# A metaformer block in software pipeline: DVE's scaling directly behind the statistics, POOL's two additions beside both, ACT's normalised columns as five in two portions

## What is computed

```python
def reference(x, conv_kernel, W1, b1, W2, b2):      # x: (32, 112, 112, 96) f32
    x = x + (conv3x3_depthwise(ln_c(x)) + ln_c(x))  # layer norm over the 96 channels, eps 1e-6
    t = to_tokens(x)
    t = t + ffn(ln_t(t))                            # layer norm over the 96 channels, eps 1e-5
    return from_tokens(t)

def ffn(t):                                         # hidden size 384
    h = relu(q_acc(q_acc(q_mul(t) @ q_mul(W1).T) + q_mul(b1)))
    return q_acc(q_acc(q_mul(h) @ q_mul(W2).T) + q_mul(b2))
```

## Time and profile before

| | before |
|---|---|
| median of 3 runs | 3998.27 us (3997.37 to 4000.93) |
| profiled execution, its own time | 3986.89 us |
| its span (first to last instruction) | 3985.2 us |
| mean granted clock of TensorE | 0.967 of full speed |
| busy: PE, DVE, ACT, POOL | 79%, 91%, 73%, 43% of the span |

### The profile page before, as it was taken

One profiled execution on the slowest core, in us unless ns is written; L12 is line 12 of the kernel. 1 busy time (PEld: TensorE's weight loads), 2 busy tenths in 40 slices (PEclk: granted clock), 3 DMA queues, 4 the chain that ended last, 5 costly groups with the idle time before them and its releaser, 6 DMA issues.

```text
span 3985.2 us, 87474 instructions
## 1 busy us (share of the span) xinstructions
PE 3157.9 (79%) x24902; PEld 2493.7 (63%) x24902; DVE 3609.6 (91%) x12635; ACT 2925.6 (73%) x6204; POOL 1719.3 (43%) x915
## 2 busy tenths in 40 slices
PE   3488888878887888878888787887888888889977
PEld 3376666666666666666666666666666666667744
DVE  6558999999999999999999899998999999999998
ACT  4457777777777777777777777777777777776765
POOL 0003444444444444444444444444444444445555
PEclk9999999999999999999999999999999999999955
DMA  4566666656666666666666666666666666665533
GB/s 135 179 175 182 189 186 189 189 173 189 189 186 187 179 185 189 186 187 189 185 189 184 181 189 186 189 186 174 189 187 189 187 189 190 191 190 171 164 107 92
DMA packets 277355, 714.63 MB, mean 179 GB/s; under 512 B 34809, under 2 KB 34914, under 8 KB 276834
## 3 DMA queue, kind: packets, MB, share of 16 engines
q1 hardware_dynamic: 276834, 708.57, 60.6%
HBM read 539.84 MB, written 168.59 MB: 178 GB/s over the span
## 4 chain that ended last, share of the span: by engine, by line
PE 54%; ACT 31%; issue 7%; DMA 4%; DVE 1%; ACTq 1%; SPq 1%; POOL 0%; POOLq 0%; DVEq 0%
PE conv_ps L390 33%; ACT images L473 14%; PE hid_ps L355 13%; ACT hid L452 9%; PE y_ps L368 7%; ACT y L460 4%; ACT xt L444 4%; DMA band_ring<-bands 3%; DMA xn<-in_x 1%; ACTq L171 1%; DVE stats L593 0%; PE conv_ps L333 0%; PE xt_ps L342 0%; DVE images L574 0%; SPq L270 0%
## 5 line engine op out<-in xcount | busy, mean ns | idle before, releaser
L390 PE MATMUL conv_ps<-images,band_ring 112*112 112x222 f32 (+1 forms) x9216 | 2058.5, 362 | 512.6 <-ACT xt L444 382.1
L390 PEld LDWEIGHTS conv_ps<-images,band_ring 112*112 112x112 f32 x9216 | 1563.0, 178 | 805.6 <-issue 550.8
L452 ACT ACTIVATE hid<-hid_ps 128x896 f16<-128x896 f32 x1344 | 1225.4, 912 | 504.4 <-PE hid_ps L355 504.4
L232 POOL TENSOR_TENSOR xf<-xf,images 112x768 f32<-112x768 f32 x448 | 979.8, 2187 | 1263.8 <-DVE hid L582 893.2
L238 POOL TENSOR_TENSOR xf<-xf,y 112x768 f32<-112x768 f32 x448 | 736.2, 1643 | 997.9 <-DVE y L613 997.9
L637 DVE SCALAR_TENSOR_TENSOR xq<-xf,stats,xt_ps 112x96 fp8e5<-112x96 f32 x3584 | 844.3, 310 | 0.0
L368 PE MATMUL y_ps<-w2t,hid 128*128 128x96 f16 x10752 | 634.7, 211 | 173.9 <-ACT y L460 172.3
L368 PEld LDWEIGHTS y_ps<-w2t,hid 128*128 128x128 f16 x10752 | 554.9, 100 | 329.3 <-ACT y L460 213.3
L473 ACT ACTIVATE images<-xn,neg_mean,rstd 112x96 f32<-112x96 f32 x1792 | 723.0, 544 | 14.3 <-DVE neg_mean L629 14.2
L355 PE MATMUL hid_ps<-xt,w1t 96*128 96x448 fp8e5 x2688 | 694.6, 368 | 27.9 <-ACT xt L444 19.4
L460 ACT ACTIVATE y<-y_ps 112x384 f16<-112x384 f32 x896 | 443.2, 495 | 363.6 <-PE y_ps L368 362.0
(11 more groups left out here) (46 smaller groups left out, 604.3 us busy)
## 6 DMA issues: line engine op xcount, KB each, us to landing
band_ring<-bands SPq DMA_DIRECT2D x768, 294.0 KB, 5.2
xn<-in_x SPq DMA_DIRECT2D x448, 336.0 KB, 3.5
xf<-in_x SPq DMA_DIRECT2D x448, 336.0 KB, 4.8
out<-xf SPq DMA_DIRECT2D x448, 336.0 KB, 3.9
bands<-images SPq DMA_DIRECT2D x4, 3528.0 KB, 13.6
xf<-in_L_ffn_W SPq DMA_DIRECT2D x2, 144.0 KB, 2.8
xf<-in_L_conv_kernel SPq DMA_DIRECT2D x3, 3.4 KB
xf<-in_L_ffn_b SPq DMA_DIRECT2D x1, 42.0 KB, 3.2
```

What stands on the lines that cost most here:

```text
L232: pool.tensor_tensor(x2, x2, images[:, b, i, :, cols].rearrange("p c w -> p w c"), ALU.add).then_inc(with_conv, 1)
L390: mm = pe.matmul(dst[:, :, lo:hi], band_ring[:, n % BAND_RING, PAIR * dx + i, :], images[:, m % 2, :, ch, lo + dx - 1:hi + dx - 1], start= ...
L452: nc.scalar.activation(hid[:, c % 2, TOK * j:TOK * (j + 1)].rearrange("p (u n) -> p u n", u=2), hid_ps[:, k, :, 0:HALF * H], ACT.Identity) ...
```

## The change

Three things are changed. No operation is added or taken out, except that one semaphore is new (`rstd_t_done`).

On DVE, `scale` of the step's own chunk comes directly behind `statistics`, with statistics and reciprocals of the step before; it was done for the next chunk, behind `invert`. `invert` is cut in two: `invert_c` (first layer norm) stands directly behind `scale`, `invert_t` (second layer norm) behind `quantise`. All three `add_bias` of chunk c - 1 stand together, in front of `quantise`. Five columns of the first layer norm are ACT's and three are DVE's (it was four and four).

On POOL, `add_ffn` comes first and takes chunk c - 3 (it was c - 2); it waits until DVE's `normalise` of the step before is done. `add_conv` follows it without a wait for DVE's biases.

On ACT, `deviation` comes first in the step, in front of `copy_xt`; two of the five columns are normalised between `copy_xt` and the first `cast_hid`, the other three between the two halves of `cast_y`. The third `cast_hid` comes in front of the first `cast_y`.

```diff
-ACT_COLS = 4
+ACT_COLS = 5
+ACT_FIRST = 2
...
-                def add_conv(r, c, t):
+                def add_conv(r, c):
...
-                    if ffn_in(t - 1):
-                        wait(pool, hid_biased, J * (LOOP * r + c - FFN_AT))
                     pool.wait_ge(xf_in[e % FFN_RING], dma_count(r, e, FFN_RING))
...
-                def add_ffn(r, c):
-                    e = c - FFN_AT
+                def add_ffn(r, c, t):
+
+                    e = c - 3 - FFN_AT
+                    if norm_in(t - 1):
+                        wait(pool, normed[1], LOOP * r + c - NORM_AT)
                     wait(pool, y_biased, LOOP * r + e + 1)
                     res = xf[0:H, e % FFN_RING]
-                    pool.tensor_tensor(res, res, y[:, c % 2], ALU.add).then_inc(summed, CW)
+                    pool.tensor_tensor(res, res, y[:, e % 2], ALU.add).then_inc(summed, CW)
 
                 def step(r, c, t):
+                    if ffn_in(t - 3):
+                        add_ffn(r, c, t)
                     if ffn_in(t + 2):
-                        add_conv(r, c, t)
-                    if ffn_in(t - 2):
-                        add_ffn(r, c - 2)
+                        add_conv(r, c)
...
-                def normalise(r, c):
+                def normalise(r, c, lo, hi):
                     e = c - NORM_AT
                     b, i, cols = chunk_at(e)
-                    wait(act, neg_done, LOOP * r + e + 1)
-                    wait(act, with_conv, LOOP * r + e - LOOP + 1)
...
+                    if lo == 0:
+                        wait(act, neg_done, LOOP * r + e + 1)
+                        wait(act, with_conv, LOOP * r + e - LOOP + 1)
...
-                    for w in range(ACT_COLS):
+                    for w in range(lo, hi):
...
+                    if ffn_in(t + 1) or norm:
+                        deviation(r, c, t)
                     if now:
                         copy_xt(r, c)
                     save_conv(r, c - 1, t - 1, 3, C)
+                    if norm:
+                        normalise(r, c, 0, ACT_FIRST)
                     if now:
                         cast_hid(r, c, 0)
-                    if ffn_in(t + 1) or norm:
-                        deviation(r, c, t)
                     save_conv(r, c, t, 0, 1)
                     if now:
                         cast_hid(r, c, 1)
                     save_conv(r, c, t, 1, 3)
+                    if now:
+                        cast_hid(r, c, 2)
                     if before:
                         cast_y(r, c - 1, 0)
-                    if now:
-                        cast_hid(r, c, 2)
                     if norm:
-                        normalise(r, c)
+                        normalise(r, c, ACT_FIRST, ACT_COLS)
                     if before:
                         cast_y(r, c - 1, 1)
...
+                def invert_t(r, c, t):
+
+                    wait(dve, xt_copied, LOOP * r + c - FFN_AT + 1 if ffn_in(t) else 0)
+                    wait(dve, std_done, LOOP * r + c - NORM_AT + 1)
+                    dve.reciprocal(rstd_t, std[:, c % 2, 0]).then_inc(rstd_t_done, 1)
...
-                    if before:
-                        add_bias(r, c - 1, 2)
+                    if now:
+
+                        wait(dve, rstd_t_done, LOOP * r + c - FFN_AT + 1)
                     if after or norm:
                         statistics(r, c, t)
...
+                    if now:
+                        scale(r, c)
+                    if norm:
+                        invert_c(r, c)
                     if before:
+                        for j in range(J):
+                            add_bias(r, c - 1, j)
                         quantise(r, c - 1)
-                    if after or norm:
-                        invert(r, c, t)
+                    if after:
+                        invert_t(r, c, t)
                     if ffn_in(t - 2):
                         add_y_bias(r, c - 2)
-                    if after:
-                        scale(r, c)
                     if norm:
                         normalise(r, c)
-                    if now:
-                        add_bias(r, c, 0)
-                        add_bias(r, c, 1)
```

More of the change, by code:

```diff
@@ L139, in metaformer @@
         stats_done, std_done, rstd_done, neg_done = sem("stats_done"), sem("std_done"), sem("rstd_done"), sem("neg_done")
+        rstd_t_done = sem("rstd_t_done")
         normed = [sem("normed_act"), sem("normed_dve")]
@@ L462, in cast_y @@
                                          ACT.Identity).then_inc(y_cast, 1)
-                def normalise(r, c):
+                def normalise(r, c, lo, hi):
                     e = c - NORM_AT
                     b, i, cols = chunk_at(e)
-                    wait(act, neg_done, LOOP * r + e + 1)
-                    wait(act, with_conv, LOOP * r + e - LOOP + 1)
-                    if e == STAGED_FROM:
-                        for s in bands_out:
-                            act.wait_ge(s, 16)
-                    for w in range(ACT_COLS):
+                    if lo == 0:
+                        wait(act, neg_done, LOOP * r + e + 1)
+                        wait(act, with_conv, LOOP * r + e - LOOP + 1)
+                        if e == STAGED_FROM:
+                            for s in bands_out:
+                                act.wait_ge(s, 16)
+                    for w in range(lo, hi):
                         op = nc.scalar.activation(images[:, b, i, :, cols.start + w], xn[:, e % NORM_RING, w, :],
@@ L475, in normalise @@
                                                   scale=rstd[:, c % 2, w:w + 1])
-                    op.then_inc(normed[0], 1)
+                    if hi == ACT_COLS:
+                        op.then_inc(normed[0], 1)
                 def save_conv(r, c, t, lo, hi):
@@ L614, in add_y_bias, with invert_c @@
                                       ALU.add).then_inc(y_biased, 1)
-                def invert(r, c, t):
+                def invert_c(r, c):
                     k = LOOP * r + c - NORM_AT
-                    if ffn_in(t + 1):
-                        wait(dve, xt_copied, LOOP * r + c - FFN_AT + 1 if ffn_in(t) else 0)
                     wait(dve, std_done, k + 1)
[L622 to L626, removed]
-                    dve.wait_ge(rstd_done, k + 1)
[L628 to L631, removed]
+                    dve.reciprocal(rstd[:, c % 2], std[:, c % 2, 1]).then_inc(rstd_done, 1)
+                    dve.wait_ge(rstd_done, k + 1)
+                    dve.scalar_tensor_tensor(out=neg_mean[:, c % 2, :], in0=stats[:, c % 2, 1, :, 1], scalar=-1.0,
+                                             in1=rstd[:, c % 2], op0=ALU.mult, op1=ALU.mult).then_inc(neg_done, 1)
+                def invert_t(r, c, t):
+                    wait(dve, xt_copied, LOOP * r + c - FFN_AT + 1 if ffn_in(t) else 0)
+                    wait(dve, std_done, LOOP * r + c - NORM_AT + 1)
+                    dve.reciprocal(rstd_t, std[:, c % 2, 0]).then_inc(rstd_t_done, 1)
                 def scale(r, c):
-                    e = c + 1 - FFN_AT
+                    e = c - FFN_AT
                     for w in range(CW):
                         op = dve.scalar_tensor_tensor(
-                            out=xq_8[:, (c + 1) % 2, w // 2, 0:C, w % 2], in0=xf[0:H, e % FFN_RING, w, :],
-                            scalar=stats[:, c % 2, 0, w, 1:2], in1=rstd_t[:, w:w + 1].broadcast_to([H, C]),
+                            out=xq_8[:, c % 2, w // 2, 0:C, w % 2], in0=xf[0:H, e % FFN_RING, w, :],
+                            scalar=stats[:, (c - 1) % 2, 0, w, 1:2], in1=rstd_t[:, w:w + 1].broadcast_to([H, C]),
                             op0=ALU.subtract, op1=ALU.mult, saturate=False)
```

3 lines of the change are left out of this document (2 added, 1 removed).

## The result

The changed kernel took 4007.65 us (median of 12 runs, 3997.93 to 4021.2), the kernel before 3997.35 beside it (12 runs). The ratio is 1.0028, with a 95% interval of 1.0015 to 1.0042: **0.28% slower**, where 0.7% faster was forecast. The profiled execution has a span of 4019.5 against 3985.2.

What follows compares the result with a forecast made beforehand. A closed chain through ACT and PE was taken to set the step, with no engine busy throughout. Terms -68 - 6 + 26 + 15 + 5 = -28 from 3998.3 gave 3970 us, range 3905 to 4040.

Steps and rivals of the forecast that it cites:

- 340 steps gain 0.20 each, -68: Loop steps: 8.12 us each instead of 8.32, taking 68 us off.
- The chain: Closed chain through DVE, PE and ACT over two steps: 16.10 us, 8.05 a step, 8.12 in the loop.
- the registers' 0.15: Working out counts in registers costs today's loop step 0.15 us; half was taken for the new chain.
- (c): Rival, chance 0.22: registers cost the loop step in full, 8.20, total 3997; with 0.2 more latency in the chain, 4036.
- The span that I gave for the forecast: 3935 to 3992 us, from unit ends at nothing or full price and a loop step of 8.05 or 8.17.
- The unit's ends: At 13 unit ends POOL's late addition holds up DVE's quantise: 2.0 us each, +26 in all.
- The closing steps: From step 419 on, y's first half stands behind the third cast: 0.27 us for 57 steps, +15.
- the first steps: In the first 28 steps ACT's fifth column lies in the chain: +5 us, at the low end nothing.
- The waits for `xn`: SP's load before the statistics: 0.7 us margin, costed at nothing; a wait there would show the prediction wrong.
- (a): Rival, chance 0.15: DVE stays out of the chain, ACT and PE alone set a 7.90 us step; total 3912.
- (b): Rival, chance 0.16: POOL meets DVE in every step when xf lands late; 4048 to 4165 us.
- `neg_mean`: DVE instruction of 0.17 us, once 1.83 beside POOL; stretching in ordinary steps would show the prediction wrong.

Runs made afterwards that it cites:

- e1: Changed kernel with unread unit-matrix matmuls in both of PE's idle places, 14 before y's second half and 12 or 6 before the transposes: 3927.03 us, ratio 0.9845.
- e2: Changed kernel with 12 or 6 unread filling matmuls only in front of the transposes: 3921.45 us, ratio 0.9818.
- e3: Changed kernel with 14 unread filling matmuls only in front of y's second half: 3920.64 us, ratio 0.982.
- e9: Kernel before with ACT's new order of casts alone, third hidden cast in front of y's first half: 3799.99 us, ratio 0.951.
- e8: Changed kernel with 14 filling matmuls before y's second half, plus ACT's square roots moved in front of y's second half: 3868.62 us, ratio 0.9683.
- e4: A follow-up that does the same as the changed kernel up to the first copy; the text ties no edit or time to this label.
- e12: Changed kernel with 14 filling matmuls before y's second half, without POOL's wait for DVE's normalise: 4755.14 us, ratio 1.1888.
- e14: Changed kernel with POOL's old code, the convolution's addition first behind its wait for the biases, then y's: 5034.88 us, ratio 1.2611.
- e15: Kernel before with ACT's new order of casts and POOL's new order, DVE's order as before: 4282.09 us, ratio 1.0724.
- e13: Changed kernel with PE's third convolution channel moved in front of y's second half, no filling matmuls: 4007.14 us, ratio 1.0041.

## Why the prediction was wrong

**The step that failed** is the first of the sum, "340 steps gain 0.20 each, -68". It takes every loop step at the full clock of its rows. By breaking PE's work with a wait for the scaling close to the wait for y, the change brings the clock down in 94 steps (14 before), which costs 95 us (122 - 27) in the profiled executions. No term and no rival stood for that; e1 to e3 give it back with steps at full clock shorter by 0.03 at most. PE's idle time in sum is not what was missing: without the loop's turns it is 1.60 a step before and 1.37 after. But before, most of it lies behind the transposes, where PE waits for the copy, with some 2 us of work between it and the idle place for y. That 4008 lies between my 3905 and 4040 is luck: two errors of opposite sign, 95 us of clock against steps at full clock that gained more than was forecast.

**The chain** was right in kind, with ACT's and DVE's small waits where I put them, and sized about 0.1 too long: 8.04 in the loop at full clock against 8.12. Half of the registers' 0.15 was right, so (c) did not come: in e3, where the clock holds, a step is 8.03 in the loop and 7.96 behind it. With the unit ends, steps at full clock gave 80 against my 68 + 6 - 26 = 48. The span that I gave for the forecast starts at 3935; with the unit ends at nothing and the step at 8.05, as I wrote there, it would start at 3920 (3970 - 26 - 24).

**The unit's ends** were right, a little dear at 2.0. In the profile after:

```profile
537.87 2.19 POOL L231 TENSOR_TENSOR xf<-xf,images 112x768 f32<-112x768 f32 x1 [3.61 <-ACT images L488]
...
538.05 2.73 DVE L595 TENSOR_SCALAR hid<-hid 128x2688 uint16<-128x2688 int16 x1
...
540.10 0.91 ACT L477 ACTIVATE images<-xn,neg_mean,rstd 112x96 f32<-112x96 f32 x2 [2.38 <-POOL xf L231]
```

That step is 9.70, 1.7 over the mean. The quantisation ends 0.72 behind POOL, as in the earlier trace rows; but ACT's first columns wait for POOL as well, which I had not seen.

**The closing steps** cost 15, as summed, but by luck: I had put all of it down to the order of the casts. That order alone (e9) makes steps 419 to 445 longer by 0.18 and the later ones by nothing, 5 us. The other 10 go when the square roots are taken earlier (e8: 7.38 to 7.19, and 6.75 to 6.57 from step 446 on), so they come from the square roots in front of the copy. That the first steps cost 4 where 5 was summed shows nothing: the first copy lies between 314.0 and 319.9 in the changed kernel and e1 to e4, which do the same up to there. The waits for `xn` from 400 to 3500 us are 0.2 in all; POOL waited 39.7 for `xf`, in 67 steps.

**Rivals.** (a) did not come: DVE is in the chain, and only e8 loosens it. (b) came in part: `quantise` is 0.86 and the biases are not stretched in ordinary steps, but `neg_mean`, whose stretching I had named as a sign that I was wrong, took 0.3 to 1.3 in 29 of the 386 steps, 12 us in all (POOL was mostly done 0.3 ahead of it, not 0.5). In the closing steps one bias in each step is longer by about 1 us beside POOL; that costs nothing that shows, since e8 has it too and its closing steps are as short as e9's. And e12, e14 and e15 show its mechanism at its full price, 0.7 to 3 us a step, as soon as POOL's order or wait is another; the Trainium skill, "SBUF — State Buffer", section "SBUF: two separate sides", has it as an exclusive lock, and these rows agree: DVE's instruction ends only behind POOL's.

**What I did not ask** is which part bears the gain. The order of casts alone is worth -198 (3800), the fifth column gives 139 of it back (3939), and DVE's and POOL's new orders, with ACT's square roots in front and its columns in two pieces, another 68 (4008), nearly all by the clock (these are steps along one path; in another order each part could be worth something else). What else in the clock's fall decides between steps with the same idle time (some 74 of 111 steps of e13 with 1.8 to 1.9 were slow) is open.

## What to carry to other kernels

When a change moves a wait of TensorE, look where its other idle times are, and read the granted clock of the steps before trusting durations taken at full speed. Take an edit of several parts to pieces first: here one moved line gave 5%, and the rest took it back. Where instructions of VectorE and GpSimd hold each other up, as in e12, e14 and e15, the orders of both are one decision.

## What the hardware showed that I had not expected

- Idle times of PE of 0.88 and 0.88 with 0.7 of work between them, or one of 1.83, were followed by half the granted clock: in the first case two whole slices of 1 us at 0.50, with 0.68 ahead of them and 0.61 behind, before it was back at 1.00. The kernel before has more idle time (1.60 a step against 1.37), spread further apart, and it happened in 4 of its steps outside the loop's turns, against 84. The Trainium skill, "TensorE: Matmul & The Clock Gate", section "A second HAM failure mode: psum-queue depth-cycling", tells of a kernel whose many short idles made the clock swing between its two levels; this trace agrees.
- Matmuls whose results nobody reads can pay: 14 more in most steps made the changed kernel 2.1% faster (ratios 0.982 and 1.0028).
- Two of POOL's additions, 1.64 and 2.19 right behind it, stretched three of DVE's columns from 0.84 to 4.13 (e12).
